# A macaron block on one core: value products of two pairs in one group, one scaled distance table, a new order of the side work, and head and tail by halves

## The chip, the cores and the metric

The kernel runs on one core of a Trainium2 chip. Its engines work at the same time and wait for each other by semaphores: PE (TensorE, matrix products and transposes into PSUM), ACT (ScalarE), DVE (VectorE), POOL (GpSimd), and SP (SyncE), which here only issues DMAs. The metric is the device time of one execution in microseconds (us), less is better.

## The reference

The input x has 16 batches of 512 rows of 128 numbers (float32). A feed-forward part with spikes, an attention part and the feed-forward part again are added to it in turn, each on the layer-normalised rows:

```
x = x + 0.5 * ffn(layernorm(x))
x = x + attention(layernorm(x))
x = x + 0.5 * ffn(layernorm(x))

ffn(u):  h = relu(u W_fc^T)^2            # 128 -> 512
         y = h W_proj^T                  # 512 -> 128
         five steps: mem = 0.9 mem + y - [mem > 1];  count += [mem > 1]
         result: count / 5
attention(u):  16 heads of 64 numbers, q scaled by 1/8
         sim = q k^T - slope[h] * |i - j|,  future positions masked
         out = softmax(sim) v;  result: out w_out + b_out
```

The slopes are 2^(-0.5 (h+1)) for head h.

## The kernel before, in words

**Tiling.** All products that must be exact are made of a high and a low half (`product3`: three matmuls on operands of type fp32r, high by high, low by high, high by low). The high half is ACT's copy out of PSUM, the low half DVE's subtraction of it from the same PSUM. The sixteen heads are worked on as eight pairs. A batch is eight slots, one for each pair `s`, and a slot is six beats `k`. In beat k the pair's scores of one entry of TILES are made (query tile i of head h against all keys up to it; for the narrow ones both heads in one bank). There are three score banks, so PE can be three tiles ahead of DVE.

**One tile's way.** PE makes the scores (`scores`, L431 and L432); DVE adds the distance bias and takes the row's minimum of the negated scores in one custom instruction (`bias_max`, L654), from a table `alibi` of 16 heads; ACT takes the exponential and the row sum (`exps`, L936); two beats later DVE takes the reciprocal of the sum (`recip`, L663) and POOL multiplies by it (`norm`, L1089). In the slot after, PE turns the pair's probabilities (`turn`, L445, five groups of four 128x128 transposes, at beats TBEAT) into two alternating banks, and ACT copies each to a ring `probT` of ten (L947). In the slot after that, PE makes the value products of the pair (`pv`, L459): for four key tiles and two heads, matmuls that write 64 output partitions each. The result's halves (ACT L954, DVE L770) enter the accumulation with w_out (`accumulate`, L514 to L517, at ACCBEAT).

**Side work.** SIDE lists what PE does besides, as (slot, beat, kind, number, batch offset): q, k and v of the next pairs, the first feed-forward part of the next batch (t1, fc1, y1), its attention input (t2), and the turned output and last part of the batch before (ot, t3, fc3, y3), and the value products ("pv", here of pair s-2, one pair in each slot). The entries use two side banks in turn, so each waits until the entry two before it has been read. In each beat PEORDER says in which order PE does side work (D), turned tiles (T) and accumulations (A), after the scores; ACTORDER does the same on ACT. The lists SPIKE1, SPIKE3, LN1, LN2 and LN3 place the steps of spikes (`spike_step`, L709 to L717) and layer norms on DVE and POOL: the stats and their aggregate on DVE (L667, L672), rstd on POOL (L1100, L1102), the normalise on DVE (L687).

**Queries and keys by DMA.** A pair's halves are copied between partitions by SP (`place`), for each pair after its q_lo and k_lo: first those for head 1, whose scores come first, then, when these have landed, those for head 0. The order of q and k in SIDE sets the order of the DMAs.

**Head.** Weights are loaded and turned, and batch 0 goes through t1, fc1, y1, the spikes and t2 with nothing beside it (`chain`, `block_by_halves` on DVE: only the spike steps are by halves of the 512 columns, the second half five steps behind the first). ACT makes the high halves of the weights and the 16 tables of `alibi` (L1050). `keep_warm` are products that nobody reads.

**Tail.** After the last slot PE makes the value products of pair 6, turns pair 7 through the two turn banks, makes its value products, accumulates, turns the output, and the last feed-forward part runs with nothing beside it.

## Time and profile before

| | us |
|---|---|
| median of 3 runs | 1609.67 (1609.4 to 1611.03) |
| the profiled execution | 1611.76 |
| its span, first to last instruction | 1610.0 |

In the profile's lists a line such as "L459" is one of the kernel's source, "x16" how often the instruction ran in a row, PEld PE's loading of weights, and what stands behind "<-" in brackets is what ended the engine's idle time before the row. Matmuls overlap: what one costs is read from the distance of two starts, not from its duration. Times of rows are from the span's start.

### The profile page before, as it was taken

To read this page: it belongs to the slowest core of one execution; us is meant where nothing else is said; L and a number is where in the kernel's file an instruction comes from. 1 tells how busy PE (TensorE), PEld (TensorE's weight loads), DVE (VectorE), ACT (ScalarE), POOL (GpSimd) and SP (SyncE) were. 2 spreads that over 40 slices of the span, in tenths; PEclk is the share of its full clock that TensorE was granted. 3 is DMA by queue.
4 is the path that set the end of the run, shared out by engine and by line. 5 is a ranking of instruction groups with operands and counts; after the bars stand their busy time and mean duration, and the time that the engine had idled before them with its cause. 6 is when DMAs were issued, how large, how long until landed. Compare 5 with 4: busy or idle time off the path is not lost.

```text
span 1610.0 us, 33997 instructions
## 1 busy us (share of the span) xinstructions
PE 1558.1 (97%) x10376; PEld 1253.8 (78%) x10376; DVE 1288.1 (80%) x4344; ACT 1312.4 (82%) x3485; POOL 954.2 (59%) x1253
## 2 busy tenths in 40 slices
PE   6899999999999999999999999999999999999996
PEld 5778778788787878778788787878778788787775
DVE  6586797878879788797878879788797878878765
ACT  6788888888888888888888888888888888888882
POOL 2555656666566666656666566666656666665551
PEclk8999999999999999999999999999999999999998
DMA  2454544444545444544444545444545444545440
GB/s 87 99 109 102 112 96 105 106 100 101 119 96 112 104 94 102 119 96 105 106 100 103 116 96 115 104 92 102 119 96 107 104 104 101 109 96 109 106 89 14
DMA packets 80052, 163.12 MB, mean 101 GB/s; under 512 B 12800, under 2 KB 30848, under 8 KB 79744
## 3 DMA queue, kind: packets, MB, share of 16 engines
q1 hardware_dynamic: 79872, 160.94, 46.4%
q8 instruction: 86, 1.41, 0.4%
q14 instruction: 94, 0.77, 0.1%
HBM read 6.88 MB, written 4.19 MB: 7 GB/s over the span
## 4 chain that ended last, share of the span: by engine, by line
PE 86%; DVE 9%; issue 2%; POOL 1%; ACT 1%; DMA 0%; POOLq 0%; DVEq 0%; SPq 0%; ACTq 0%
PE bank L445 16%; PE bank L459 14%; PE bank L431 11%; PE bank L432 10%; PE bank L411 7%; PE bank L415 7%; PE bank L412 7%; PE bank L504 7%; DVE xn L687 3%; PE bank L487 2%; PE bank L517 2%; PE bank L515 2%; PE bank L514 2%; DVE negsc L654 2%; POOL rstd L1102 1%
## 5 line engine op out<-in xcount | busy, mean ns | idle before, releaser
L1089 POOL TENSOR_TENSOR prob<-prob,rsum 128x512 f32<-128x512 f32 (+3 forms) x1024 | 769.9, 767 | 489.5 <-DVE rsum L663 486.9
L936 ACT ACTIVATE prob<-negsc,negmax 128x512 f32<-128x512 f32 (+3 forms) x1024 | 574.4, 563 | 165.7 <-DVE negmax L654 163.3
L654 DVE CUSTOM_DVE_ANT_0 negsc<-bank,alibi 128x512 f32<-128x512 f32 (+3 forms) x1024 | 466.9, 475 | 0.3 <-PE bank L432 0.3
L947 ACT COPY probT<-bank 128x512 f32<-128x512 f32 x640 | 352.0, 584 | 27.5 <-PE bank L445 21.4
L445 PE MATMUL bank<-ident,prob 128*128 128x128 f32 x2560 | 350.9, 273 | 0.8 <-POOL prob L1089 0.5
L431 PE MATMUL bank<-keys,queries 128*128 128x256 f32 (+2 forms) x1024 | 348.6, 351 | 0.3
L663 DVE RECIPROCAL rsum<-sums 128x1 f32<-128x1 f32 (+1 forms) x768 | 122.3, 159 | 260.1 <-PE bank L432 248.0
L432 PE MATMUL bank<-keys,queries 128*128 128x256 f32 (+2 forms) x1024 | 320.0, 324 | 0.0
L445 PEld LDWEIGHTS bank<-ident,prob 128*128 128x128 f32 x2560 | 299.4, 140 | 24.0 <-POOL prob L1089 0.7
L459 PE MATMUL bank<-probT,vals 128*64 128x512 f32 (+3 forms) x2048 | 303.9, 439 | 3.3 <-DVE queries L778 2.5
L459 PEld LDWEIGHTS bank<-probT,vals 128*64 128x64 f32 x2048 | 135.6, 136 | 163.6 <-issue 125.2
L431 PEld LDWEIGHTS bank<-keys,queries 128*128 128x128 f32 x1024 | 193.5, 189 | 33.1 <-issue 18.2
L432 PEld LDWEIGHTS bank<-keys,queries 128*128 128x128 f32 x1024 | 194.2, 190 | 15.1
L936 ACT ACTIVATION_READ_ACCUMULATOR prob<-negsc,negmax 128x1 f32 x1024 | 196.1, 191 | 0.0
L1095 POOL TENSOR_TENSOR hid<-hid 128x512 f32<-128x512 f32 x120 | 124.9, 1041 | 23.6 <-ACT hid L994 23.5
L504 PE MATMUL bank<-wproj,hid 128*128 128x128 f32 x1024 | 125.1, 275 | 0.3 <-DVE k_lo L785 0.3
L504 PEld LDWEIGHTS bank<-wproj,hid 128*128 128x128 f32 x1024 | 121.4, 192 | 2.7 <-DVE k_lo L785 0.7
L954 ACT CAST att_hi<-bank 128x512 fp32r<-128x512 f32 x128 | 74.8, 585 | 38.3 <-PE bank L459 37.5
L785 DVE TENSOR_TENSOR k_lo<-bank,keys 128x512 fp32r<-128x512 f32 x127 | 87.5, 689 | 8.5 <-ACT keys L969 7.9
L770 DVE TENSOR_TENSOR att_lo<-bank,att_hi 128x512 fp32r<-128x512 f32 x128 | 87.7, 685 | 5.2 <-ACT att_hi L954 5.2
L711 DVE SCALAR_TENSOR_TENSOR spikes<-negmem,spikes 128x512 f32<-128x512 f32 (+1 forms) x136 | 91.2, 673 | 0.8
L778 DVE TENSOR_TENSOR queries<-bank,queries 128x512 fp32r<-128x512 f32 x127 | 86.3, 680 | 4.6 <-ACT queries L969 4.0
(108 smaller groups left out, 2421.0 us busy)
## 6 DMA issues: line engine op xcount, KB each, us to landing
queries<-queries SPq DMA_DIRECT2D x381, 256.0 KB, 3.0
keys<-k_lo SPq DMA_DIRECT2D x254, 128.0 KB, 2.7
keys<-keys SPq DMA_DIRECT2D x127, 128.0 KB, 3.1
x_in<-in_L_attn_x_dram SPq DMA_DIRECT2D x16, 256.0 KB, 3.1
out_dram<-x SPq DMA_DIRECT2D x15, 256.0 KB, 3.6
prob<-in_L_attn_w_qkv_dram SPq DMA_DIRECT2D x1, 1536.0 KB, 9.4
prob<-in_L_attn_w_out_dram SPq DMA_DIRECT2D x1, 512.0 KB, 10.2
probT<-in_L_ffn_W_fc_dram SPq DMA_DIRECT2D x1, 256.0 KB, 3.3
```

The costliest lines, as they stand in the source:

```text
L411: pe.matmul(dst, w_hi, m_hi, start=True, stop=False)
L431: pe.matmul(dst, q_hi[:, p % 2, h, rows], keys[:, p % 2, h, 0:width], start=True, stop=False)
L432: mm = pe.matmul(dst, q_lo[:, p % 2, h, rows], keys[:, p % 2, h, 0:width], start=False, stop=True)
L445: mm = pe.transpose(turn_bank[n % 2][:, col:col + P], prob[:, p % 2, h, PCOL[i] + j * P:PCOL[i] + (j + 1) * P], ident[:, :])
L459: mm = pe.matmul(bank[h * DH:(h + 1) * DH, j * P:N], vals[:, (p // 2) % 2, j, (p % 2) * P + h * DH:(p % 2) * P + (h + 1) * DH], probT[:, t ...
L504: mm = pe.matmul(dst[:, t * C:(t + 1) * C], hid[:, i, rows], wproj[:, i, :], start=(i == 0 and t == 0), stop=(i == FC - 1), skip_group_che ...
L654: ins = dve.tensor_tensor_reduce(negsc[:, k % 3, col:col + WIDTH[i]], src, alibi[:, 2 * p + h, N - WIDTH[i]:N], 1.0, MASKED, ALU.add, ALU.min,
L663: dve.reciprocal(rsum[:, p % 2, cols], sums[:, p % 2, cols]).then_inc(s_rsum, 1)
L936: ins = act.activation(prob[:, p % 2, h, PCOL[i]:PCOL[i] + WIDTH[i]], negsc[:, k % 3, col:col + WIDTH[i]], ACT.Exp, bias=negmax[:, p % 2, ...
L947: act.copy(probT[:, turn_slot(p, t), :], turn_bank[(len(TRUNS) * p + t) % 2][:, :]).then_inc(s_turned_out, 1)
L1089: ins = pool.tensor_tensor(pr, pr, rsum[:, p % 2, seg:seg + 1].to_broadcast([P, WIDTH[i]]), ALU.mult)
L1095: pool.tensor_tensor(hid[:, i, :], hid[:, i, :], hid[:, i, :], ALU.mult).then_inc(s_hid[w], 1)
```

## The change

Value products: `pv` stands twice at one beat of the odd slots, for pairs s-3 and s-2, in place of once in every slot, and the ring `probT` has 20 places in place of ten. The distance table: one table `dist`, to which the scores are added; q's weights are divided by the head's slope beforehand and DVE's instruction multiplies by the slope. The order of side work, turned tiles, accumulations, spikes and layer norms is new. In head and tail the feed-forward part runs by halves of 256 columns on all engines, the squares of the second half on POOL; the second half of the spikes is seven steps behind. In the tail the last five turned tiles go to five banks, two of them are copied by DVE, and the last pair's value products, accumulation and output turn are by halves. The core of the diff:

```diff
-TRING = 10
+TRING = 20
 TBEAT = [
-    [1, 2, 2, 5, 5],
-    [1, 1, 3, 3, 5],
-    [1, 1, 4, 5, 5],
-    [1, 2, 4, 5, 5],
-    [1, 2, 2, 5, 5],
-    [0, 2, 3, 4, 5],
-    [1, 1, 4, 5, 5],
-    [1, 1, 3, 3, 5],
+    [1, 2, 3, 4, 4],
+    [1, 4, 4, 5, 5],
+    [1, 4, 4, 5, 5],
+    [1, 1, 4, 4, 5],
+    [3, 3, 4, 5, 5],
+    [0, 2, 2, 5, 5],
+    [1, 1, 4, 4, 5],
+    [0, 2, 2, 5, 5],
 ]
-ACCBEAT = [7, 6, 6, 6, 6, 6, 11, 11]
-OUTEV = (2, 1)
+ACCBEAT = [11, 15, 6, 17, 8, 11, 6, 8]
+OUTEV = (2, 3)
...
 SIDE = [
-    (0, 0, "q", 0, 0), (0, 1, "k", 0, 0), (0, 2, "v", 0, 0), (0, 4, "pv", 0, 0), (0, 4, "v", 1, 0),
-    (0, 5, "t1", 0, 1),
-    (1, 0, "q", 0, 0), (1, 1, "k", 0, 0), (1, 2, "fc1", 0, 1), (1, 4, "fc1", 1, 1), (1, 4, "pv", 0, 0),
-    (1, 5, "fc1", 2, 1),
-    (2, 0, "fc1", 3, 1), (2, 0, "k", 0, 0), (2, 1, "ot", 0, -1), (2, 2, "y1", 0, 1), (2, 3, "q", 0, 0),
-    (2, 4, "y1", 1, 1), (2, 4, "pv", 0, 0), (2, 5, "v", 0, 0), (2, 5, "t3", 0, -1),
-    (3, 0, "q", 0, 0), (3, 1, "k", 0, 0), (3, 3, "v", 1, 0), (3, 4, "pv", 0, 0), (3, 5, "fc3", 0, -1),
-    (4, 0, "k", 0, 0), (4, 1, "q", 0, 0), (4, 3, "v", 0, 0), (4, 4, "pv", 0, 0), (4, 5, "v", 1, 0),
-    (4, 5, "fc3", 1, -1),
-    (5, 0, "q", 0, 0), (5, 1, "k", 0, 0), (5, 3, "fc3", 2, -1), (5, 4, "pv", 0, 0), (5, 5, "fc3", 3, -1),
-    (6, 0, "k", 0, 0), (6, 1, "y3", 0, -1), (6, 1, "q", 0, 0), (6, 3, "y3", 1, -1), (6, 4, "pv", 0, 0),
-    (6, 4, "t2", 0, 1),
-    (7, 0, "q", 0, 1), (7, 1, "v", 0, 0), (7, 2, "k", 0, 1), (7, 3, "pv", 0, 0), (7, 4, "v", 1, 0),
+    (0, 0, "q", 0, 0), (0, 1, "v", 0, 0), (0, 2, "v", 1, 0), (0, 2, "k", 0, 0), (0, 3, "t1", 0, 1),
+    (0, 5, "fc1", 0, 1), (0, 5, "fc1", 1, 1),
+    (1, 1, "q", 0, 0), (1, 2, "k", 0, 0), (1, 4, "pv", 0, 0), (1, 4, "pv", 1, 0),
+    (2, 0, "q", 0, 0), (2, 1, "fc1", 2, 1), (2, 2, "k", 0, 0), (2, 3, "fc1", 3, 1), (2, 4, "v", 2, 0),
+    (2, 4, "ot", 0, -1),
+    (3, 0, "v", 3, 0), (3, 0, "k", 0, 0), (3, 1, "q", 0, 0), (3, 3, "pv", 0, 0), (3, 3, "pv", 1, 0),
+    (3, 5, "v", 4, 0),
+    (4, 0, "y1", 0, 1), (4, 0, "k", 0, 0), (4, 1, "y1", 1, 1), (4, 1, "t3", 0, -1), (4, 2, "q", 0, 0),
+    (4, 3, "fc3", 0, -1), (4, 4, "fc3", 1, -1), (4, 5, "fc3", 2, -1), (4, 5, "v", 5, 0),
+    (5, 1, "k", 0, 0), (5, 1, "q", 0, 0), (5, 3, "fc3", 3, -1), (5, 4, "pv", 0, 0), (5, 4, "pv", 1, 0),
+    (6, 0, "q", 0, 0), (6, 0, "k", 0, 0), (6, 3, "y3", 0, -1), (6, 3, "v", 6, 0), (6, 4, "y3", 1, -1),
+    (6, 4, "t2", 0, 1), (6, 5, "v", 7, 0),
+    (7, 1, "q", 0, 1), (7, 2, "k", 0, 1), (7, 4, "pv", 0, 0), (7, 4, "pv", 1, 0),
 ]
-SPIKE1 = [(2, 4), (3, 2), (3, 4), (3, 4), (4, 0), (4, 1), (4, 2), (4, 4), (4, 5), (5, 0), (5, 4), (5, 4), (6, 0), (6, 1)]
-SPIKE3 = [(6, 4), (6, 4), (7, 0), (7, 1), (7, 1), (7, 2), (7, 3), (7, 3), (7, 5), (8, 4), (9, 0), (9, 1), (9, 2), (9, 4)]
-LN1 = dict(stats=(0, 0), aggregate=(0, 3), rstd=(0, 3), normalise=(0, 4))
-LN2 = dict(stats=(6, 1), aggregate=(6, 2), rstd=(6, 2), normalise=(6, 4))
-LN3 = dict(stats=(2, 2), aggregate=(2, 4), rstd=(2, 4), normalise=(2, 4))
+SPIKE1 = [(4, 2), (4, 3), (4, 3), (4, 4), (4, 5), (4, 5), (4, 5), (4, 5), (5, 1), (5, 2), (5, 2), (5, 3), (5, 3), (5, 4)]
+SPIKE3 = [(7, 1), (7, 1), (7, 4), (7, 4), (7, 4), (8, 2), (8, 3), (8, 5), (9, 1), (9, 2), (9, 3), (9, 4), (9, 4), (9, 4)]
+LN1 = dict(stats=(0, 0), aggregate=(0, 1), rstd=(0, 2), normalise=(0, 2))
+LN2 = dict(stats=(5, 4), aggregate=(6, 2), rstd=(6, 3), normalise=(6, 4))
+LN3 = dict(stats=(3, 0), aggregate=(3, 1), rstd=(3, 1), normalise=(3, 2))
 FIRST = [(1, "q"), (1, "k"), (0, "q"), (0, "k")]
...
+        def pv_pair(b, s, i):
+            return before(b, s, 3 - i)
...
+        def last_turn_bank(t):
+            return turn_bank[(len(TRUNS) * (PAIRS - 1) + t) % 2] if t < 2 else score_bank[t - 2]
+        LAST_BY_VECTOR = (2, 4)
+        def acc_at(p):
+            return divmod((p - p % 2 + 3) * BEATS + ACCBEAT[p], BEATS)
         def score_col(k, n):
...
+            def block_by_halves(w, b, made):
+                e = 0 if w == 1 else 1
+                first = s_first_half
+                def turn_half(half):
+                    pe.wait_ge(*((first["xn"], e + 1) if half == 0 else (s_xn[w], b + 1)))
+                    for t in range(half * NT // 2, (half + 1) * NT // 2):
+                        mm = pe.transpose(end_turn_bank[half][:, t * P:(t + 1) * P], xn[:, t, :], ident[:, :])
+                    mm.then_inc(first["xT"] if half == 0 else s_xT[w], 1)
+                def fc_half(i, half):
+                    cols, rows = HALVES[half], slice(i * P, (i + 1) * P)
+                    low_made = None
+                    if i == 0:
+                        pe.wait_ge(*((first["xhi"], e + 1) if half == 0 else (s_xhi[w], b + 1)))
+                        low_made = (first["xlo"], e + 1) if half == 0 else (s_xlo[w], b + 1)
+                    if half == 1:
+                        pe.wait_ge(first["relu"], e * FC + i + 1)
+                    product3(end_fc_bank[i][:, cols], wfc_hi[:, rows], wfc_lo[:, rows], xf_hi[:, cols], xf_lo[:, cols],
+                             low_made).then_inc(first["fc"] if half == 0 else s_fc[w], 1)
+                def y_half(half):
+                    for i in range(FC):
+                        pe.wait_ge(*((first["hid"], e * FC + i + 1) if half == 0 else (s_hid[w], b * FC + i + 1)))
+                        for t in range(2):
+                            rows = slice((2 * half + t) * P, (2 * half + t + 1) * P)
+                            mm = pe.matmul(end_y_bank[half][:, t * C:(t + 1) * C], hid[:, i, rows], wproj[:, i, :],
+                                           start=(i == 0 and t == 0), stop=(i == FC - 1), skip_group_check=True)
+                    mm.then_inc(s_y[w], 1)
+                turn_half(0)
+                turn_half(1)
+                if made:
+                    pe.wait_ge(*made[0])
+                for i in range(FC):
+                    fc_half(i, 0)
+                if made:
+                    pe.wait_ge(*made[1])
+                y_half(0)
+                for i in range(FC):
+                    fc_half(i, 1)
+                y_half(1)
             def head():
...
                         keep_warm(6)
-                chain(0, ("t1",))
-                keep_warm(5)
-                pe.wait_ge(s_wfc_lo, 1)
-                chain(0, ("fc1",))
-                pe.wait_ge(s_wproj_out, 1)
-                chain(0, ("y1",))
-                pe.wait_ge(s_x1, 1)
-                keep_warm(9)
-                chain(0, ("t2",))
-                keep_warm(5)
+                block_by_halves(1, 0, ((s_wfc_lo, 1), (s_wproj_out, 1)))
+                pe.wait_ge(s_block_half, 1)
+                keep_warm(9, score_bank[1])
+                for half in range(2):
+                    pe.wait_ge(*((s_first_half["xn2"], 1) if half == 0 else (s_xn[2], 1)))
+                    for t in range(2 * half, 2 * half + 2):
+                        mm = pe.transpose(end_turn_bank[half][:, t * P:(t + 1) * P], xn[:, t, :], ident[:, :])
+                    mm.then_inc(s_first_half["xT2"] if half == 0 else s_xT[2], 1)
+                    keep_warm(3, score_bank[1])
...
+            def last_turn(t):
+                b, p = B - 1, PAIRS - 1
+                pe.wait_ge(s_norm, tile_no(b, p, TNEEDS[t]))
+                if t < 2:
+                    pe.wait_ge(s_turned_out, turn_no(b, p, t - 2))
+                elif t == 2:
+                    pe.wait_ge(s_biased, tile_no(b, p, BEATS - 1))
+                col = 0
+                for h, j in TRUNS[t]:
+                    for i in range(j, NT):
+                        mm = pe.transpose(last_turn_bank(t)[:, col:col + P],
+                                          prob[:, p % 2, h, PCOL[i] + j * P:PCOL[i] + (j + 1) * P], ident[:, :])
+                        col += P
+                mm.then_inc(s_turned, 1)
+            def last_pv(half):
+                b, p, end = B - 1, PAIRS - 1, HALVES[half].stop
+                pe.wait_ge(s_turned_out, turn_no(b, p, len(TRUNS) - 1))
+                pe.wait_ge(s_vals, v_no(b, p // 2, 1))
+                for j in range(2 * half + 2):
+                    start = max(j * P, HALVES[half].start)
+                    for h in range(2):
+                        t, col = place_of(h, j)
+                        mm = pe.matmul(last_pair_bank[half][h * DH:(h + 1) * DH, start:end],
+                                       vals[:, (p // 2) % 2, j, (p % 2) * P + h * DH:(p % 2) * P + (h + 1) * DH],
+                                       probT[:, turn_slot(p, t), col + start - j * P:col + end - j * P], start=(j == 0),
+                                       stop=(j == 2 * half + 1), skip_group_check=True)
+                mm.then_inc(s_pv, 1)
+            def last_accumulate(half):
+                b, p, cols = B - 1, PAIRS - 1, HALVES[half]
+                pe.wait_ge(s_att, pair_no(b, p) + half)
+                if half == 1:
+                    pe.wait_ge(s_outT, B)
+                pe.matmul(out_bank[:, cols], wo_hi[:, p, :], att_hi[:, p % 2, cols], start=False, stop=False, skip_group_check=True)
+                pe.matmul(out_bank[:, cols], wo_lo[:, p, :], att_hi[:, p % 2, cols], start=False, stop=False, skip_group_check=True)
+                pe.wait_ge(s_attlo, pair_no(b, p) + half)
+                pe.matmul(out_bank[:, cols], wo_hi[:, p, :], att_lo[:, p % 2, cols], start=False, stop=True,
+                          skip_group_check=True).then_inc(s_acc, 1)
+            def last_out_turn(half):
+                pe.wait_ge(s_outT, B + half)
+                for t in range(half * NT // 2, (half + 1) * NT // 2):
+                    mm = pe.transpose(turn_bank[half][:, t * P:(t + 1) * P], outT[:, t * P:(t + 1) * P], ident[:, :])
+                mm.then_inc(s_out, 1)
...
                     wait(pe, *last_user(len(SIDE) - (len(SIDE) - n) % 2, b, (-1, 0)))
-                for back in (3,):
-                    if ACCBEAT[PAIRS - 1] >= BEATS:
-                        accumulate(b, PAIRS - 3)
+                for p in range(PAIRS - 2):
+                    if acc_at(p) >= (PAIRS, 0):
+                        accumulate(b, p)
                 for j in PVORDER:
                     pv(side_bank[0], *six, j)
-                for t in range(3):
-                    turn(*seven, t)
+                for t in range(len(TRUNS)):
+                    last_turn(t)
+                for half in range(2):
+                    last_pv(half)
                 accumulate(*six)
-                for t in range(3, len(TRUNS)):
-                    turn(*seven, t)
-                for j in PVORDER:
-                    pv(side_bank[1], *seven, j)
-                keep_warm(6, score_bank[0])
-                accumulate(*seven)
-                keep_warm(4, score_bank[0])
-                out_turn(turn_bank[0], b)
-                keep_warm(16)
-                chain(b, ("t3",))
-                keep_warm(5)
-                chain(b, ("fc3", "y3"))
+                for half in range(2):
+                    last_accumulate(half)
+                    last_out_turn(half)
+                keep_warm(14, score_bank[1])
+                block_by_halves(3, b, None)
...
-                                                   alibi[:, 2 * p + h, N - WIDTH[i]:N], 1.0, MASKED, ALU.add, ALU.min,
+                                                   dist[:, N - WIDTH[i]:N], SLOPES[2 * p + h], MASKED, ALU.add, ALU.min,
...
+            def normalise_by_halves(w, src, b):
+                e = 0 if w == 1 else 1
+                dve.wait_ge(s_rstd[w], b + 1)
+                if w == 3:
+                    dve.wait_ge(s_xT[1], B)
+                    dve.wait_ge(s_xT[2], B)
+                for t in range(NT):
+                    ins = dve.tensor_scalar(xn[:, t, :], src[:, t, :], meanvar[:, w - 1, t, 0:1],
+                                            rstd[:, w - 1, t:t + 1], ALU.subtract, ALU.mult)
+                    if t == 1:
+                        ins.then_inc(s_first_half["xn"], 1)
+                ins.then_inc(s_xn[w], 1)
+                for half, cols in enumerate(HALVES):
+                    dve.wait_ge(*((s_first_half["xhi"], e + 1) if half == 0 else (s_xhi[w], b + 1)))
+                    dve.tensor_tensor(xf_lo[:, cols], end_turn_bank[half][:, cols], xf_hi[:, cols].bitcast(F32),
+                                      ALU.subtract).then_inc(s_first_half["xlo"] if half == 0 else s_xlo[w], 1)
+                for i in range(FC):
+                    dve.wait_ge(s_first_half["relu"], e * FC + i + 1)
+                    part = hid[:, i, HALVES[0]]
+                    dve.tensor_tensor(part, part, part, ALU.mult).then_inc(s_first_half["hid"], 1)
             def head():
...
+                for t in LAST_BY_VECTOR:
+                    dve.wait_ge(s_turned, turn_no(b, PAIRS - 1, t))
+                    dve.wait_ge(s_pv, pv_no(b, PAIRS - 5, NT - 1))
+                    dve.tensor_copy(probT[:, turn_slot(PAIRS - 1, t), :], last_turn_bank(t)[:, :]).then_inc(s_turned_out, 1)
...
-                chain(0, ("t1", "fc1", "y1"))
+                ends_by_halves(1, 0)
                 act.wait_ge(s_wqkv, 16)
-                act.mul(wq_hi[:, :], w_raw[:, 0:INNER], -SCALE).then_inc(s_whi, 1)
+                for h in range(HEADS):
+                    cols = slice(h * DH, (h + 1) * DH)
+                    ins = act.mul(w_raw[:, cols], w_raw[:, cols], -SCALE / SLOPES[h])
+                ins.then_inc(s_scaled, 1)
+                act.wait_ge(s_scaled, 1)
+                act.copy(wq_hi[:, :], w_raw[:, 0:INNER]).then_inc(s_whi, 1)
...
                 act.wait_ge(s_wlo, 1)
                 copy_twice("q", 1, wq_lo)
-                chain(0, ("t2",))
...
+            def square_second(w, b):
+                for i in range(FC):
+                    pool.wait_ge(s_relu[w], b * FC + (i + 1))
+                    half = hid[:, i, HALVES[1]]
+                    pool.tensor_tensor(half, half, half, ALU.mult).then_inc(s_hid[w], 1)
...
```

## Rows read from the trace of the kernel before

**Rows 1.** page, part 1: busy us, share of the span and instructions of each engine

```profile
PE 1558.1 (97%) x10376; PEld 1253.8 (78%) x10376; DVE 1288.1 (80%) x4344; ACT 1312.4 (82%) x3485; POOL 954.2 (59%) x1253
```

**Rows 2.** windows: stage, its us, busy us of each engine, granted clock, DMA share, GB/s

```profile
36.52:73.62 37.10, 31.94 (x191) 26.70 (x190) 21.30 (x86) 25.89 (x70) 21.02 (x27) 0.91 0.42 89
...
225.35:321.86 96.51, 95.63 (x644) 76.96 (x642) 79.93 (x270) 80.88 (x217) 59.72 (x79) 1.00 0.49 105
248.49:263.61 15.12, 15.12 (x112) 13.00 (x110) 10.22 (x40) 11.40 (x32) 9.96 (x14) 1.00 0.32 70
...
1570.10:1610.00 39.90, 26.03 (x183) 20.32 (x181) 23.70 (x62) 10.59 (x25) 4.99 (x8) 0.90 0.05 14
```

**Rows 3.** timeline of PE around one value group: start us, us, instruction

```profile
485.54 0.60 PE L445 MATMUL bank<-ident,prob 128*128 128x128 f32 x4
486.07 2.37 PE L459 MATMUL bank<-probT,vals 128*64 128x512 f32 x16
488.37 0.39 PE L431 MATMUL bank<-keys,queries 128*128 128x256 f32 x1
488.60 0.28 PE L432 MATMUL bank<-keys,queries 128*128 128x256 f32 x1
488.71 0.28 PE L431 MATMUL bank<-keys,queries 128*128 128x256 f32 x1
...
492.29 1.05 PE L445 MATMUL bank<-ident,prob 128*128 128x128 f32 x8
493.17 1.95 PE L504 MATMUL bank<-wproj,hid 128*128 128x128 f32 x16
```

**Rows 4.** waits, 200 to 1400 us: us in total, times, longest

```profile
PE bank L487 <- DVE xn L687: 9.2, 13, 0.7
...
PE bank L487 <- DVE att_lo L770: 2.2, 13, 0.2
```

**Rows 5.** timelines of PE, DVE and POOL around t2, 398 to 407 us

```profile
405.81 0.63 PE L487 MATMUL bank<-ident,xn 128*128 128x128 f32 x4 [0.71 <-DVE xn L687]
403.16 2.51 DVE L687 TENSOR_SCALAR xn<-x,meanvar,rstd 128x128 f32<-128x128 f32 x4
400.99 0.20 POOL L1100 TENSOR_TENSOR vareps<-meanvar,eps 128x4 f32<-128x4 f32 x1 [2.39 <-DVE meanvar L672]
...
402.25 2.82 POOL L1089 TENSOR_TENSOR prob<-prob,rsum 128x512 f32<-128x512 f32 x3
```

**Rows 6.** timeline of the head: the normalise of t2

```profile
29.34 1.11 DVE L687 TENSOR_SCALAR xn<-x,meanvar,rstd 128x128 f32<-128x128 f32 x4 [1.19 <-POOL rstd L1102]
```

**Rows 7.** DMA issues with KB and us to landing; and part 5's group of k_lo

```profile
keys<-k_lo SPq DMA_DIRECT2D x198, 128.0 KB, 2.7
...
L785 DVE TENSOR_TENSOR k_lo<-bank,keys 128x512 fp32r<-128x512 f32 x127 | 87.5, 689 | 8.5 <-ACT keys L969 7.9
```

**Rows 8.** waits, 1500 to 1515 us, in the last batch

```profile
PE bank L459 <- DVE queries L778: 1.5, 1, 1.5
PE bank L411 <- DVE x L758: 1.1, 1, 1.1
```

**Rows 9.** head: one row of the timeline, then of the chain: start us, us

```profile
21.70 8.42 ACT L1050 ACTIVATE alibi<-probT 128x512 f32<-128x512 f32 x16
15.24 0.38 ACT ysb L1003
...
25.43 0.42 DVE x L731
```

**Rows 10.** chain of the tail

```profile
1585.21 0.46 PE bank L523 x4
...
1589.11 1.12 DVE xn L687 x4
...
1597.06 0.38 ACT ysb L1003
...
1599.87 0.20 DVE spikes L709
```

273 lines of the change are left out of this document (171 added, 102 removed).

## The prediction

> **What bounds the kernel now.** I read the page's busy shares first, then the windows by stage, then PE's timeline around one value group, then the waits, the chain of the first 37 us and of the last 40 us. PE is busy 97% of the span [rows 1]. A steady batch takes 96.5 us, of which PE is busy 95.6 at full granted clock, DVE 79.9, ACT 80.9, POOL 59.7 [rows 2]: PE bounds the loop, the others follow within a tile or so, and a change is worth what it takes from PE's own time or from its idle moments. Three stretches have other limits: the head (to 36.5 us, a chain through all engines), the first slots (36.5 to 73.6, PE busy 31.9 of 37.1 us at a granted clock of 0.91) and the last 39.9 us, where PE is busy 26.0 [rows 2].
>
> **Value products of two pairs in one group.** These matmuls write 64 output partitions each, all others 128. Their 16 matmuls have 2 x 2 x (512+384+256+128) = 5120 columns, 2.13 us at 2.4 GHz, the level of this stretch (granted clock 1.00). From [rows 3]: start to start the group takes 488.37 - 486.07 = 2.30, 0.17 too much. The four transposes before it take 486.07 - 485.54 = 0.53, while eight elsewhere take 493.17 - 492.29 = 0.88, so four should take 0.44: 0.09 too much. The first 256-wide score after it takes 0.23, the next ones 0.11: 0.12 too much. In all 0.38. Some of the 0.17 may belong to the matmuls and not to the change of shape, so the bounds are 0.21 (nothing inside the group) and 0.38; the sum over the two borders is what repeats in every group, so I take 0.35. Going in and out is paid once per group. There are 128 groups now (8 pairs x 16 batches). After, the pairs go two by two at beats (1,4), (3,3), (5,4), (7,4): 3 groups in the first batch, 4 in each of the other 15, and two in the tail, 65. 63 x 0.35 = 22.1 us less (13 to 24).
>
> The Trainium skill ("TensorEngine Tiling (Array Packing)", Key Properties) says that changing the tiling mode, not just the tile, drains the engine. By that rule the pair boundary inside a double group costs nothing, since both pairs use the same mode. No row of this trace shows two such groups back to back.
>
> **The moved side work.** Each kind of side unit has as many entries as before (8 q, 8 k, 8 v, 4 fc1, ...), so PE's work is the same but for the borders. What changes is who waits. (a) PE waits at t2 for the normalised rows: 9.2 us in 13 batches, and at t1 for att_lo: 2.2 us in 13 [rows 4], 0.88 us a batch. At t2 DVE's normalise took 2.51 us for four tiles [rows 5], while in the head, with POOL idle, four take 1.11 [rows 6]. In between POOL ran three softmax scalings back to back, 2.82 us, because it had waited 2.39 us for meanvar at the rstd step just before [rows 5]. The change puts the aggregate one beat before rstd, so that backlog goes: one scaling (2.82 / 3 = 0.94) is left beside the normalise. DVE starts at 403.16 as before; 402.25 + 0.2 + 0.94 = 403.4, + 1.11 = 404.5, + 0.14 (405.81 less the end of the normalise, 405.67) = 404.6. PE arrives at t2 after two turned tiles (0.88) and a y unit (1.7 to 1.8, in place of the group's 2.30 and one turned tile), from 402.2 at about 404.9. So the t2 wait goes; with the old contention it would be 0.9. I take 0.1. At t1 the normalise now stands at (0,2) and t1 at (0,3), with no value group between them. Counted from the end of the group at (7,4), PE issues five tiles of scores up to there, five turned tiles, two accumulations, q, k and two v: 8.6 us (0.11 for 128 columns, 0.12 for 256 [rows 3], twice that for 512). DVE gets its scores at 2.8 and has three biases, stats, aggregate, q's low half and a spike step before the normalise, four wide ones of about 0.65 (k_lo's took 0.69 with its start-up [rows 7]) and smaller ones: 4.3, so it starts at 7.1; with 0.35 for one scaling on POOL, 1.11 and 0.14 the rows are ready at 8.7, and at 9.7 with 2.51 in place of 1.11 and no 0.35: a wait of 0.1 to 1.1, and 0 to 1.3 with my error in 15 operations. I take 0.4, near the lower end, because POOL has then one scaling to do. Sum 0.5 a batch in place of 0.88: 15 x 0.4 = 6 us less (13 less to 20 more).
> (b) In even slots there is no group now, and slot 2 falls from 15.1 [rows 2] to about 10 us (a group and two y units, 6, leave it); odd slots keep PE 4.6 us from the scores. Three score banks lie between PE and DVE. Spike steps are heaped: four at (4,5), finish and LN2 stats at (5,4). Over those beats DVE has up to 3 us more work than PE; before it is about 1.6. A third bank allows about two beats of 2 us, so I take no stall; up to 1 us a batch (15) is kept for the range.
> (c) k moves to beat 2 in slots 0, 1, 2 and 7, so its low half and the copy to the other partitions start later before the next pair's scores. A copy of k_lo takes 2.7 us to land, and DVE's subtraction 0.69 [rows 7]. In slot 2 PE does scores of three tiles, fc1, four turned tiles, v and ot after k: 4.9 us. The chain is a copy on ACT of about the same 0.7, DVE 0.9 with its bias ahead, DMA 2.7: 4.4 us with the semaphores. It just fits. It is SP's queue: the q copies stand ahead of k's where q comes first.
> (d) In the last batch PE waited 1.1 us for x2 and 1.5 for queries behind it [rows 8], since `ot` stood one beat after the accumulation of pair 7. Now ACT copies at (2,3) and `ot` stands at (2,4), behind a v: 2.6 less (0 to 3).
> (e) The first batch: slots 0 to 2 lose a group and two y units (2.3 + 3.6 us of PE work) to later slots, where PE is full, while PE idles here (5.2 of 37.1 us [rows 2]). Against that t1's wait is shorter by about 2 us and so is the slow clock behind it. I take 0 (3 less to 4 more).
>
> **DVE's bias operation** is the same instruction with a scale other than 1.0 and another second operand of the same size: 0 (nothing in it changes length). The 16 products that made the table took ACT 8.42 us of the head [rows 9]; in their place come 16 narrow ones on w_raw (estimate 4 us, half as long, each a fixed part and an eighth of the width) and one more 1024-wide copy (about 1 us). ACT's 3 us less matter only if ACT is last there.
>
> **Head.** Now: y's first half leaves ACT at 15.62, x1 is done at 25.85 [rows 9], scores start at 36.5 [rows 2]. By halves: fc on 256 columns halves the time to the first y: ready about 13.6, 2.0 earlier. But the second half's squares go to POOL, beside DVE's spike steps. Four squares of half width (0.6 each, estimated from 0.94 for a wide POOL operation [rows 5]) alternating with DVE's steps of 0.42 [rows 9]: second half ready at 17 to 18.5, and 13 steps and two sums later, of which six pairs interleave at 0.67 and seven stand alone, x1 is done at 24.4 to 26.1. LN2 by halves saves 0.5, the low-half subtraction of q and k for one pair only instead of two of 1.2 us saves about 1. I take 3.5 less (1 to 5).
>
> **Tail.** Five banks let the five last turned tiles follow without waiting for copies, two of the copies go to DVE: now the out turn is at 1585.21, rows normalised by 1590.23, y's first half at 1597.44, second spike half at 1599.87 [rows 10]. From the last score: the out turn about 1.5 to 2 earlier; fc and y by halves 3 earlier for the first half, but the store waits for the second, which has POOL's squares in it. From its start to the end stays 10 us. One accumulation (0.7) moves into the tail. 3.8 less (1 to 6).
>
> On POOL beside DVE: normalise took 2.51 against 1.11 [rows 5, 6]. The Trainium skill ("SBUF — State Buffer", SBUF: two separate sides) says the port pair that both share is an exclusive lock, held for a whole instruction. The trace agrees. By it the squares and spike steps in head and tail alternate and the second halves gain almost nothing: then head and tail give 2 us together, not 7.3.
>
> **Sum**, against the profiled execution's own 1611.8 us (span 1610.0): 22.1 + 6 + 2.6 + 0 + 3.5 + 3.8 = 38.0 less, 1573.8. The median of the runs shown is 2.1 below the profiled one: 1571.7, say 1572.
>
> **Rivals.**
> A, the new order adds waits: t1 at its upper bound (1.3 + 0.9 at t2, 1.3 more than now) or the DVE heap of (4,5): for it, DVE's excess nearly doubles; against it, DVE waits for PE now in most beats. +1 us a batch instead of -0.4: 21 more than forecast, 1593. Chance 0.17.
> B, the group's borders are cheaper to PE than counted or also paid between pairs (the change doesn't do what it says): 22 less gain, 1594. Against it: one row has both borders outside the group. 0.05.
> C, slower than before: the copy chain of (c) becomes the bound. If k_lo lands 3.7 instead of 2.7 us after issue and DVE is 1 us late, the next pair's scores wait 1.5 us in each of slots 0 and 2, from the point where the chain passes 4.9 us. To be slower it must cost over 38 / 15 = 2.5 us a batch; 3 gives 1572 + 45 = 1617. For it: the slack is 0.5 us. Against: a late PE also gives DVE time. 0.05.
> D, PE waits nowhere in the loop and the halves bring all: 15 x 0.5 more and 4 in head and tail, 1560. 0.15.
> By the lock rule of the page alone: 5 us above the forecast, 1577, inside it.
>
> **Numbers.** The forecast (1565 to 1583) has 0.58. Range 1558 to 1595: it takes in A, B and D. This kernel's measurement tells 0.2%, about 3.2 us, from no change. Faster by more: 0.93; within: 0.02; slower: 0.05.
>
> **What would show it.** PE's value groups in x32 with 4.4 to 4.6 us each and one slow first score behind them; a steady batch of 94.4 to 95; PE's wait for normalised rows under 0.3 us at t2; the first score at about 33; the last 40 us at 36 to 37. Wrong if PE's waits for DVE or for the copies grow past 1 us a batch, or the borders don't shrink in number.

## The result, and the profile after

The changed kernel takes 1626.13 us (median of 4, 1625.4 to 1627.7), the kernel before in the same session 1609.86: a ratio of 1.0100 (95% interval 1.0087 to 1.0114), 1.0% slower. The forecast was 1572, so 54 us are missing. The forecast's own signs of being wrong came true: PE's waits grew by 1.74 us a batch, where 1 was the sign, and a steady batch is 97.4 us long instead of 94.4 to 95. The profiled execution has a span of 1625.9 us against 1610.0, and 15.9 is what has to be explained.

By the first scores of each batch the span divides into (before, after): up to the first scores 36.52, 35.26; the first batch 92.3, 97.3; batches 2 to 15 1351.6, 1363.6 (96.54 and 97.40 each); the last batch to its slot 7 80.3, 80.3; the rest 49.2, 49.4. The head gained 1.3 and the tail lost 0.2; what was lost, was lost in the loop, 5.0 in the first batch and 12.0 in the next 14, where about 28 were forecast to be gained.

First the page's busy times (compare [rows 1]), then the windows by stage ([rows 2]): its us, then busy us of PE, PEld, DVE, ACT and POOL, granted clock, DMA share, GB/s. The third window is no stage of the forecast: it is beats (4,3) to (5,4) of batch 6.

```profile
PE 1554.5 (96%) x10365; PEld 1255.0 (77%) x10365; DVE 1281.2 (79%) x4353; ACT 1292.1 (79%) x3496; POOL 976.7 (60%) x1263
```

```profile
35.26:72.36 37.10, 29.90 (x162) 24.58 (x163) 21.78 (x91) 27.27 (x76) 23.95 (x32) 0.91 0.46 96
228.80:326.01 97.21, 95.31 (x644) 77.15 (x641) 79.51 (x269) 79.87 (x218) 61.07 (x78) 1.00 0.48 103
573.00:590.00 17.00, 16.24 (x98) 12.60 (x98) 16.83 (x43) 13.05 (x34) 12.18 (x13) 1.00 0.42 91
...
1586.00:1625.90 39.90, 25.53 (x177) 20.44 (x175) 27.88 (x70) 10.32 (x27) 7.91 (x11) 0.88 0.05 14
```

DVE has no more to do in a batch than before, 79.5 us of 97.2; of the other engines only POOL is clearly busy longer (61.1 us, before 59.7), because some of its operations now take longer. But in the 17 us from (4,3) to (5,4) DVE is busy 16.83; before it was busy 12.25 in the 15.0 us from 569.0, the same beats. Over a batch it has 18 us to spare, here none. That is the place, and the waits of PE from 200 to 1400 us say the same (in total, times, longest; before, two groups of them, 9.2 and 2.2 us [rows 4]):

```profile
PE bank L465 <- POOL prob L1287: 10.0, 12, 1.1
PE bank L479 <- ACT hid L1161: 4.6, 13, 0.4
PE bank L507 <- DVE xn L793: 3.7, 12, 0.3
PE bank L451 <- issue: 3.1, 5, 1.0
PE bank L537 <- DVE att_lo L878: 2.8, 9, 0.3
```

Slots and beats in brackets are those of PE's order. For a finer ledger I took, for batches 2 to 15, each distance between two starts on PE less the distance usual for that form, where it exceeds 0.15 us, by slot and beat. Before: 0.77 us a batch at t2 (6,4), 0.34 at t1 (0,5), 1.13 in all. After: **1.02 at (5,2)**, where a turned tile (L465) waits for POOL's scaled probabilities; **0.52 at (5,4)**, where the second pair's products (L479) wait for ACT's `hid` to free their bank; 0.44 at t1 (0,3); 0.30 at (2,0), accumulate on att_lo; 0.57 for landings of copied queries and keys ahead of scores (the profile calls most of them "issue"); 2.87 in all. So 1.74 more in waits and 1.4 less in borders; the batch is 0.86 longer, and the 0.5 between is what follows a wait (a remainder, not measured).

How the wait at (5,2) comes about, in one batch: DVE, then POOL, then PE (start, us, instruction, idle before).

```profile
577.59 1.07 DVE L817 SCALAR_TENSOR_TENSOR spikes<-negmem,spikes 128x512 f32<-128x512 f32 x1
...
579.07 1.04 DVE L820 SCALAR_TENSOR_TENSOR drive<-negmem,ysb 128x512 f32<-128x512 f32 x1
580.15 1.20 DVE L823 SCALAR_TENSOR_TENSOR negmem<-negmem,drive 128x512 f32<-128x512 f32 x1
581.38 1.41 DVE L817 SCALAR_TENSOR_TENSOR spikes<-negmem,spikes 128x512 f32<-128x512 f32 x1
582.72 0.68 DVE L820 SCALAR_TENSOR_TENSOR drive<-negmem,ysb 128x512 f32<-128x512 f32 x1
583.32 0.15 DVE L769 RECIPROCAL rsum<-sums 128x2 f32<-128x2 f32 x1
```

```profile
578.08 1.49 POOL L1293 TENSOR_TENSOR hid<-hid 128x512 f32<-128x512 f32 x1
579.53 1.27 POOL L1287 TENSOR_TENSOR prob<-prob,rsum 128x384 f32<-128x384 f32 x1
580.76 1.48 POOL L1293 TENSOR_TENSOR hid<-hid 128x512 f32<-128x512 f32 x1
583.55 1.18 POOL L1287 TENSOR_TENSOR prob<-prob,rsum 128x256 f32<-128x256 f32 x2 [1.31 <-DVE rsum L769]
```

```profile
584.79 1.09 PE L465 MATMUL bank<-ident,prob 128*128 128x128 f32 x8 [0.65 <-POOL prob L1287]
```

The four spike steps of beat (4,5) (579.07 to 582.72) stand ahead of the reciprocal at 583.32. One takes 0.68 us where POOL idles (582.72) and 1.04 to 1.41 beside POOL's operations, which are stretched too: the squares (L1293) have a mean of 1.30 us against 1.04 before. POOL then waits 1.31 us for the reciprocal, and PE for POOL. The rows show the two taking turns: each of the three long steps ends 0.54 or 0.55 us after an operation of POOL ends (579.57, 580.80 and 582.24). Before, spike steps and squares seldom met: from 200 to 1400 us 12 of 300 steps overlapped a square, after 84 of 293. In these lists the shortest, median and longest duration in ns stand behind the count; before, then after:

```profile
L711 DVE SCALAR_TENSOR_TENSOR spikes<-negmem,spikes x100: 673/684/730, 201.5 to 1390.9; 128x512 f32<-128x512 f32 x100
L1095 POOL TENSOR_TENSOR hid<-hid x97: 1036/1041/1047, 203.0 to 1361.6; 128x512 f32<-128x512 f32 x97
```

```profile
L817 DVE SCALAR_TENSOR_TENSOR spikes<-negmem,spikes x98: 674/693/1417, 200.8 to 1394.6; 128x512 f32<-128x512 f32 x98
L1293 POOL TENSOR_TENSOR hid<-hid x97: 1034/1487/1492, 202.7 to 1371.4; 128x512 f32<-128x512 f32 x97
```

The border, the one large gain, came as forecast: two pairs in 270.90 - 266.45 = 4.45 us, less than twice the 2.30 that one group took before [rows 3]: the change from one pair to the next costs nothing.

```profile
266.45 4.53 PE L479 MATMUL bank<-probT,vals 128*64 128x512 f32 x32
270.90 0.39 PE L451 MATMUL bank<-keys,queries 128*128 128x256 f32 x1
271.13 0.28 PE L452 MATMUL bank<-keys,queries 128*128 128x256 f32 x1
```

In the first batch PE waits longest at the end of slot 1, first SP's issue, then PE. The copy of k_lo (subtracted at 51.16) is issued at 52.50 behind the queries' and the high half's, and the scores start at 57.51; after that idle time the granted clock is 0.50 (1.2 GHz) for the 5.5 us to 63.0. The low clock is not new: over the first slots the mean is 0.91 before and after.

```profile
52.50 1.23 SPq L373 DMA_DIRECT2D keys<-k_lo  x1
```

```profile
52.56 1.12 PE L465 MATMUL bank<-ident,prob 128*128 128x128 f32 x8 [1.03 <-ACT probT L1114]
57.51 0.77 PE L451 MATMUL bank<-keys,queries 128*128 128x512 f32 x1 [3.84 <-issue]
```

The chain of the tail ([rows 10]): the output is turned at 1598.42, yet x2 comes at 1601.07, behind five steps left over of batch 15's third block. DVE had idled 3.08 us up to 1592.71, waiting for turned tiles of PE; experiment 4 takes them there.

```profile
1597.59 0.59 DVE spikes L817
...
1600.35 0.70 DVE x L829
1601.07 0.43 DVE x L1074
...
1611.34 0.37 ACT ysb L1203
...
1616.38 0.29 DVE spikes L815
```

### The profile page after: what moved, and what is told of

It reads as the page before. It is cut to its first block, busy times and chain, and to the rows that moved or that the text cites. A ratio compares the mean times of both kernels' runs of the same rounds, so it can differ in the third digit from the quotient of the medians.

```text
span 1625.9 us, 33995 instructions
## 1 busy us (share of the span) xinstructions
PE 1554.5 (96%) x10365; PEld 1255.0 (77%) x10365; DVE 1281.2 (79%) x4353; ACT 1292.1 (79%) x3496; POOL 976.7 (60%) x1263
## 3 DMA queue, kind: packets, MB, share of 16 engines
q8 instruction: 86, 1.41, 0.4%
## 4 chain that ended last, share of the span: by engine, by line
PE 67%; DVE 21%; issue 5%; ACT 4%; DMA 1%; POOL 0%; SPq 0%; DVEq 0%; ACTq 0%; POOLq 0%
PE bank L479 13%; PE bank L465 11%; PE bank L451 8%; PE bank L452 7%; PE bank L524 7%; PE bank L431 5%; PE bank L435 5%; PE bank L432 5%; DVE negsc L760 4%; DVE drive L820 3%; DVE spikes L817 3%; ACT prob L1103 3%; DVE negmem L823 2%; DVE xn L793 2%; PE bank L537 2%
## 5 line engine op out<-in xcount | busy, mean ns | idle before, releaser
L1287 POOL TENSOR_TENSOR prob<-prob,rsum 128x512 f32<-128x512 f32 (+3 forms) x1024 | 756.0, 754 | 570.4 <-DVE rsum L769 570.0
L760 DVE CUSTOM_DVE_ANT_0 negsc<-bank,dist 128x512 f32<-128x512 f32 (+3 forms) x1024 | 466.6, 474 | 0.1
L465 PE MATMUL bank<-ident,prob 128*128 128x128 f32 x2540 | 344.4, 274 | 13.1 <-POOL prob L1287 11.9
L465 PEld LDWEIGHTS bank<-ident,prob 128*128 128x128 f32 x2540 | 293.0, 140 | 41.0 <-POOL prob L1287 23.3
L479 PE MATMUL bank<-probT,vals 128*64 128x512 f32 x2032 | 290.7, 436 | 5.2 <-ACT hid L1161 5.0
L479 PEld LDWEIGHTS bank<-probT,vals 128*64 128x64 f32 x2032 | 135.6, 137 | 156.2 <-issue 117.0
L1103 ACT ACTIVATION_READ_ACCUMULATOR prob<-negsc,negmax 128x1 f32 x1024 | 202.7, 198 | 0.0
L1293 POOL TENSOR_TENSOR hid<-hid 128x512 f32<-128x512 f32 x120 | 155.1, 1297 | 0.3 <-ACT hid L1161 0.3
L524 PE MATMUL bank<-wproj,hid 128*128 128x128 f32 x960 | 116.9, 275 | 0.0
L524 PEld LDWEIGHTS bank<-wproj,hid 128*128 128x128 f32 x960 | 114.9, 192 | 1.3
L817 DVE SCALAR_TENSOR_TENSOR spikes<-negmem,spikes 128x512 f32<-128x512 f32 (+1 forms) x136 | 113.8, 837 | 2.4
L886 DVE TENSOR_TENSOR queries<-bank,queries 128x512 fp32r<-128x512 f32 x127 | 86.9, 684 | 15.9 <-ACT queries L1136 15.0
L823 DVE SCALAR_TENSOR_TENSOR negmem<-negmem,drive 128x512 f32<-128x512 f32 (+1 forms) x102 | 94.1, 922 | 0.7
```

What stands on the lines that cost most here:

```text
L465: mm = pe.transpose(turn_bank[n % 2][:, col:col + P], prob[:, p % 2, h, PCOL[i] + j * P:PCOL[i] + (j + 1) * P], ident[:, :])
L479: mm = pe.matmul(bank[h * DH:(h + 1) * DH, j * P:N], vals[:, (p // 2) % 2, j, (p % 2) * P + h * DH:(p % 2) * P + (h + 1) * DH], probT[:, t ...
L524: mm = pe.matmul(dst[:, t * C:(t + 1) * C], hid[:, i, rows], wproj[:, i, :], start=(i == 0 and t == 0), stop=(i == FC - 1), skip_group_che ...
L760: ins = dve.tensor_tensor_reduce(negsc[:, k % 3, col:col + WIDTH[i]], src, dist[:, N - WIDTH[i]:N], SLOPES[2 * p + h], MASKED, ALU.add, AL ...
L817: ins = dve.scalar_tensor_tensor(out=spikes[:, cols], in0=mem[:, cols], scalar=sign * THRESHOLD, in1=spikes[:, cols], op0=fires, op1=ALU.add)
L823: ins = dve.scalar_tensor_tensor(out=negmem[:, cols], in0=mem[:, cols], scalar=sign * THRESHOLD, in1=drive[:, cols], op0=fires, op1=ALU.su ...
```

## The experiments

Ratios are to the kernel before. "Heap" is the pile of spike steps at (4,5), "mended ends" the fourth run's edit. Lines start with the kernel's own names, edits are to the changed kernel.

**1. The borders.** One product of 128 columns on the full array, between the two pairs.

```diff
                 elif kind == "pv":
+                    if i == 1:
+                        pe.matmul(side_bank[n % 2][:, 0:P], ident[:, :], ident[:, :], start=True, stop=True)
                     for j in PVORDER:
                         pv(bank or side_bank[n % 2], *pv_pair(b, s, i), j)
```

> Edit: the changed kernel with one full-array product of 128 columns put between the two pairs' value products of every double group, which gives back the border that the change removed; nothing else is changed (63 of them). Border theory: a border in and out costs 0.35 us beside the product's own 0.10: 63 x 0.45 = 28 us more than the changed kernel, less what falls into waits that stand right behind it: 1648 to 1656 us, ratio 1.024 to 1.029, and the second pair's first gap is again 0.42 us and more. Rival, borders overlap with other work or with the weight load: only the product's own time, 63 x 0.10 = 6 us, 1630 to 1634.

1646.81 us, 1.0226 (1.0211 to 1.0241), 20.7 more than the changed kernel. That is less than expected, since PE's waits fell from 2.87 to 2.25 a batch. The timeline shows the border itself. From 200 to 1400 us the stretch from the first value product to the next score grew from 4.46 to 5.03 us in the 37 of 49 double groups that hold no wait, by 0.57:

```profile
248.49 2.37 PE L479 MATMUL bank<-probT,vals 128*64 128x512 f32 x16
250.80 0.49 PE L565 MATMUL bank<-ident 128*128 128x128 f32 x2
251.22 2.38 PE L479 MATMUL bank<-probT,vals 128*64 128x512 f32 x16
253.52 0.38 PE L451 MATMUL bank<-keys,queries 128*128 128x256 f32 x1
```

The product is two records (x2). In the tail of the changed kernel 14 such products stand in a row, 28 records whose starts are 0.11 apart:

```profile
1599.96 3.29 PE L572 MATMUL bank<-ident 128*128 128x128 f32 x28
```

So the product itself is 0.22 (the expectation counted 0.10), and the border 0.57 - 0.22 = 0.35. The forecast's 0.35 stands, and the gain of about 22 us was there and was spent.

**2. Spreading the heap.**

```diff
-SPIKE1 = [..., (4, 4), (4, 5), (4, 5), (4, 5), (4, 5), (5, 1), (5, 2), (5, 2), (5, 3), (5, 3), (5, 4)]
+SPIKE1 = [..., (4, 4), (4, 5), (4, 5), (5, 1), (5, 2), (5, 3), (5, 4), (5, 4), (5, 4), (5, 5), (5, 5)]
-LN2 = dict(stats=(5, 4), ...
+LN2 = dict(stats=(6, 1), ...
```

> Edit: in the changed kernel the first block's spike steps are spread (two of the four at (4,5) move to (5,1), the rest follow down to (5,5)) and the second LayerNorm's statistics move from (5,4) to (6,1). Heap theory: the PE waits at (5,2) (turned tile on the normalised probabilities, 1.02 us a batch) and (5,4) (second value pair's group on the hidden half, 0.52) come from the pile of spike steps on VectorE between 4,5 and 5,2, each stretched by GpSimd's squares beside it (1.04 to 1.41 us where one takes 0.68 alone). Then both waits go, 1.5 us a batch, and with their followers up to 1.9: 15 batches give 20 to 28 us; some of it comes back as new waits further on. Expected 1600 to 1610 us, ratio to before 0.995 to 1.000. Rival, total load: VectorE and GpSimd have too much to do in the second half of the batch and the pile only moves: 1624 to 1630, waits of the same sum at (5,5) to (6,4).

1627.27 us, 1.0111 (1.0094 to 1.0128): nothing gained. (5,2) fell to 0.14 and (5,4) to nothing, but 0.56 came at (6,1), 0.56 at t2 and 0.49 at (6,4) for a bank; 2.82 in all. The rival was right on the total.

```profile
PE bank L507 <- DVE xn L793: 8.5, 24, 0.4
PE bank L465 <- POOL prob L1287: 5.6, 15, 0.4
PE bank L524 <- ACT ysb L1170: 4.2, 13, 0.3
```

**3. Earlier queries and keys.** Slot 1: q (1,0), k (1,1); slot 2: k (2,1), fc1 (2,2).

> Edit: in slots 1 and 2 of the changed kernel the query and key tiles are made one beat earlier (slot 1: q at beat 0, k at beat 1; slot 2: k at beat 1, the third fc tile at beat 2). Copy theory: the key copies made by DMA from GpSimd's k_lo land 3.8 to 5 us after their issue, so with k at beat 2 the next slot's first scores wait for them: 0.44 us a batch at the ends of slots 1 and 2, and 4.0 us in the first batch at the end of slot 1, after which TensorE runs at the lower clock for some 6 us. Then 0.4 x 15 = 6 and in the first batch 4 to 6 more: 1614 to 1618 us, ratio 1.003 to 1.006. Rival, GpSimd: k_lo is late because GpSimd is still at the squares and attention remainders, so an earlier tile on TensorE changes nothing there: 1624 to 1628, waits at the same places.

1634.46 us, 1.0147 (1.0131 to 1.0162), 8 slower. That is outside both theories. The first batch gained 3.5 us, as the copy theory had it, and has no stretch at half clock in its first slots. A steady batch lost 0.61: PE waits 0.80 instead of 0.30 at (2,0) for att_lo. The last batch lost 3.2, with 6.8 us at a granted clock of 0.50 from 1548.4. (k_lo is made by DVE, not by GpSimd as the expectation says.)

**4. The ends.**

```diff
-                for n in spilled[:2]:
+                for n in spilled[:6]:
...
+                weights_low(1, wk_hi, wk_lo, others, s_wrest)
                 norm2_normalise(1)
-                weights_low(1, wk_hi, wk_lo, others, s_wrest)
+                weights_low(0, wq_hi, wq_lo, others, s_wrest)
```

> Edit: the ends of the changed kernel alone. In the head the rest of the key weights' remainders is subtracted ahead of the second half's normalise and the query weights' right behind it (they stood behind the second half's remainders of x, beside GpSimd's 3.3 us on the value weights, and one of them took 2.54 us). In the tail the spike steps left over are taken while VectorE is idle (six instead of two ahead of the last pair, the last ones right behind). Theory: head 1.5 to 2.5 us earlier (first scores at 33 to 34 instead of 35.26), tail 1.5 to 3 (x2 no longer at 1601.07 behind five steps): 1620.5 to 1623, ratio 1.006 to 1.009. Rival: what ends last in the head is the value weights on GpSimd, and in the tail the last turned tiles: 1625 to 1627.

1619.42 us, 1.0061 (1.0046 to 1.0076). The tail is 3.0 us shorter, as expected. The head is not shorter (first scores 35.2): the subtraction moved beside POOL's rstd, which took 1.43 us instead of 0.69, and the normalise waited for it. The first batch is 2.0 shorter and the steady ones 0.3 each, where only landings of copies differ; this I can't ascribe to the edit.

**5. Is it DVE's load?** On the mended ends; nothing is moved. The rest of six spike steps' columns in each steady batch is left out of the computation.

```diff
+                elif w == 1 and n > 3 and n % 3 != 0:
+                    cols = slice(0, 2)
```

> Edit: the changed kernel with the mended ends (1619.4 us), where six of the first block's fourteen spike steps in each steady batch (drive and membrane of the last three times) work on 2 columns instead of 512; the place and the order of everything stay. The rest of their columns is left out of the computation. It tells whether VectorE's load in slots 4 and 5 is what TensorE waits for at (5,2) and (5,4). Load theory: about 6 x 0.8 us less on VectorE before (5,4), more where GpSimd's squares stretch them; the waits at (5,2) 1.03 and (5,4) 0.52 a batch go, with 0.3 of followers: 1.5 to 1.9 us a batch, 1592 to 1598. Rival, GpSimd itself (squares of the third block ahead of its normalising, 1.3 us each): (5,2) stays for the most part, 1608 to 1616.

1591.69 us, 0.9881 (0.9865 to 0.9898), 27.7 less. The waits at (5,2) and (5,4) are gone, a steady batch takes 95.3 us, and three kinds of wait are left:

```profile
PE bank L507 <- DVE xn L793: 4.1, 13, 0.3
PE bank L537 <- DVE att_lo L880: 3.1, 10, 0.3
PE bank L451 <- issue: 2.9, 6, 1.0
```

POOL's squares were all still there, so the rival falls: DVE's load between (4,2) and (5,4) costs 1.85 us a batch. (This is the price of the load of the six steps where they stand, their turns with POOL included; the run doesn't divide the two. The kernel before has the same fourteen steps and no such wait.)

**6. y of the first block earlier.** Two value tiles go to slot 4 for it; one spike step to a beat from (3,3).

```diff
-    (3, 0, "v", 3, 0), (3, 0, "k", 0, 0), (3, 1, "q", 0, 0), (3, 3, "pv", 0, 0), (3, 3, "pv", 1, 0),
-    (3, 5, "v", 4, 0),
-    (4, 0, "y1", 0, 1), (4, 0, "k", 0, 0), (4, 1, "y1", 1, 1), (4, 1, "t3", 0, -1), ...
+    (3, 0, "y1", 0, 1), (3, 0, "k", 0, 0), (3, 1, "q", 0, 0), (3, 2, "y1", 1, 1), (3, 3, "pv", 0, 0), ...
+    (4, 0, "v", 3, 0), (4, 0, "k", 0, 0), (4, 1, "v", 4, 0), (4, 1, "t3", 0, -1), ...
```

> Edit: the changed kernel with the mended ends, and in it the first block's two y tiles a slot earlier (slot 3, beats 0 and 2, in the place of two value tiles, which go to slot 4), so that its fourteen spike steps stand one to a beat from (3,3) to (5,4); before this edit they stood from (4,2) to (5,4), in the kernel before from (2,4) to (6,1). Window theory (what is left of the heap theory after spreading within slots 4 and 5 had only moved the waits): the new order has put y of the first block so late that VectorE has 14 spike steps and the rest of its work in the 12 beats before the turned tile of the second LayerNorm at (6,4), and is behind whatever their order. With 27 beats as before it is not: the waits at (5,2), (5,4) and those that the spread moved to (6,1) and (6,4) go, 1.5 to 1.8 us a batch, 15 batches: 22 to 28 us less than 1619.4, so 1591 to 1598, ratio 0.989 to 0.993. Rival, GpSimd: the wait at (5,2) comes from the squares of the third block standing ahead of the normalising, and stays (1.0 us a batch): 1606 to 1613.

1648.47 us, 1.0239 (1.0217 to 1.0261). The theory's gain came, and a larger loss with it. The waits at (5,2), (5,4) and (6,4) went, and slot 5 fell from 14.2 to 12.7 us. But 2.36 a batch came at (4,1): a value tile wants the bank of the one two entries before, ACT has still to copy it, and ACT stands behind an exponential that waits for DVE. PE, then ACT:

```profile
580.88 0.39 PE L430 MATMUL bank<-wv_hi,xa_hi 128*128 128x256 f32 x1 [2.19 <-ACT vals L1141]
```

```profile
579.54 0.72 ACT L1102 ACTIVATE prob<-negsc,negmax 128x512 f32<-128x512 f32 x1 [0.84 <-DVE negmax L759]
...
580.26 0.56 ACT L1141 COPY vals<-bank 128x512 f32<-128x512 f32 x1
```

**7. The same with the banks set apart** (y at (3,0) and (3,1), q (3,2); slot 4: k, t3 and v, q), later third spikes.

> Edit: the mended ends, the late spike steps of the third block as in the run before this one, and the first block's y tiles at (3,0) and (3,1), its spike steps one to a beat from (3,3) to (5,4). In the first try of early y tiles two value tiles one beat apart had the same bank, and the second stood 2.36 us a batch waiting for ScalarE's copy of the first; here no two tiles of one bank are closer than that order had them elsewhere. What the first try had shown else: slot 5 12.7 us instead of 14.2 and no waits at (5,2), (5,4) or (6,4). Window theory: left are 4.96 less 2.36, 0.32, 0.24 and 0.5 of their followers, less 0.7 for the later spike steps: 0.9 us a batch, so 95.3 us a batch, 1590 to 1597, ratio 0.987 to 0.992. Rival, banks: with both side banks taken by a double group and two tiles needed in each beat of slots 3 and 4, some pair of tiles always meets; the wait moves to another tile of slots 3 and 4 (1 to 2 us a batch): 1610 to 1630.

1718.14 us, 1.0673 (1.0654 to 1.0692): the rival, and several times dearer than it said. The ledger has 8.17 us a batch, most of it for banks held until DVE's subtraction: 1.88 and 1.72 at (4,1) and (4,2), 1.51 at (3,3) ahead of the double group. Not all of it is waiting. PE's idle time is 5.9 a batch; most of the rest is PE at half clock, for 3.4 to 10.2 us in every steady batch, which no steady batch of the mended ends has:

```profile
600.00:606.80 6.80, 5.34 (x17) 4.24 (x18) 3.04 (x10) 2.22 (x5) 1.40 (x2) 0.50 0.18 39
```

From 200 to 1400 us the mean granted clock is 0.97, against 1.00 with the mended ends: about 3 of the 6.7 us that a batch lost (an estimate, 0.03 of 103.8). In experiment 6 it is 0.99.

**8. The double groups in the old order.** On the mended ends, with TBEAT, PEORDER, ACTORDER, the spikes and the first and second layer norms at the beats of the kernel before; only both pairs' products in the odd slots, `ot` at (2,4), t3 at (3,5); the accumulations and the first fc3 tile, at (4,2), moved with them.

> Edit: the grouping without the new order. The changed kernel with the mended ends, but the side work, the turned tiles, the order on TensorE and ScalarE, the spike steps and the first and second LayerNorms stand in the beats of the kernel before; only what the grouping forces is moved (both pairs' value products in slots 1, 3, 5 and 7, the output tile at (2,4), the turned tile of the third LayerNorm at (3,5)). Theory: the grouping itself is worth its borders, 1.4 us a batch, and the new order is what loses: then 1609.7 less 21, less 2 to 6 at the ends, plus what the waits at the double groups bring: 1582 to 1592, ratio 0.983 to 0.989. Rival, grouping itself is at fault: products for two pairs in one beat leave the other engines 2.1 us more to make up at a time, and the waits appear in this order too: 1605 to 1625.

1823.62 us, 1.1322 (1.1305 to 1.1338). This is the largest miss of the experiments, on the far side of both theories: 15.3 us of waits a batch.

```profile
PE bank L505 <- DVE xn L791: 44.2, 22, 2.3
PE bank L429 <- DVE att_lo L876: 22.3, 33, 0.8
PE bank L449 <- DMA queries<-queries: 20.2, 22, 1.4
```

The second line is the grouping's own: a double group fills both side banks, so an fc tile one beat behind it, (1,5) or (5,5), stands until att_lo is subtracted, 0.99 us each. The old order had a tile there, with one bank free. So the grouping can't simply be put into the old order; how the rest divides (xn at 2.5 and 1.85 a batch) these runs don't tell.

**9. Small moves.** The third block's steps from the sixth on later ((8,3), ..., the last two (9,5)), and keys of slots 1 and 2 at beat 1; then, without the keys, those steps and the last fc3 tile at (5,2); then with the heap spread, LN2 at (6,0) to (6,3) and y3 at (6,2) as well.

> Edit: the changed kernel with the mended ends (1619.4 us), and the small waits alone: the third block's last eight spike steps later (its sixth at (8,3) instead of (8,2), so behind the first LayerNorm's normalise; the last two at (9,5) instead of (9,4), so behind the remainder of the attention's output), the keys of slot 1 at beat 1 behind the queries, those of slot 2 at beat 1 with the fc tile behind them. Theory: each of the waits at (0,3) (0.44 a batch), (2,0) (0.35), and the late key copies (0.1 a batch, 2.75 us in the first batch) goes by itself: 0.9 x 15 + 3 = 16, so 1601 to 1606, ratio 0.995 to 0.998. Rival, waits move on to the next wait of TensorE, which stays at (5,2): a batch keeps 97.1 us, 1615 to 1619.

> Edit: the mended ends; the third block's spike steps from the sixth on as in the run with the three small waits (the sixth at (8,3), the last two at (9,5)), keys left where the change has them; and the third block's last fc tile at (5,2) instead of (5,3). In the run with the three small waits the spike steps had taken the waits at (0,3) and (2,0) away, and the earlier keys had brought 1.02 us a batch back at (2,2) and (2,3), where an fc tile waits for the bank of the tile two before it. Theory: without those keys 0.44 + 0.35 a batch stay gone, and the wait at (5,4) for the fc tile's bank (0.52) shrinks: 0.8 to 1.3 x 15 = 12 to 20 us less than 1619.4: 1600 to 1607. Rival, banks: the fc tile at (5,2) waits for the bank of the key tile of (5,1), 0.5 to 1.0 a batch: 1607 to 1615.

> Edit: as the run before this one, and the first block's spike steps spread down to (5,5) with no more than three in a beat, the second LayerNorm's steps at (6,0), (6,1), (6,2) and (6,3), and the third block's first y tile at (6,2) instead of (6,3). Spreading alone had taken 0.9 off the wait at (5,2) and brought 0.56 at (6,1), 0.56 at (6,4) for the second LayerNorm's x and 0.49 at (6,4) for a bank. Theory: with the LayerNorm a beat earlier and the y tile's bank free sooner the last two do not come: 0.5 to 1.5 us a batch less than the run before: 1585 to 1600. Rival, VectorE is behind by a fixed amount until (6,4) because y of the first block stands late (27 beats for its spike steps in the kernel before, 13 here): the waits stay 1.5 us a batch in sum wherever they fall, 1600 to 1610.

1627.45 us, 1.0101 (1.0082 to 1.0120); 1639.37, 1.0176 (1.0161 to 1.0191); 1627.50, 1.0098 (1.0080 to 1.0116). In each the wait aimed at went (t1's 0.44 in all; t2's and (6,1)'s in the third) and others came for banks: 0.64 and 0.38 at (2,2) and (2,3) in the first; about 1 at (5,2) for the bank of the key tile one beat before in the second and third; 0.98 at (6,2) in the third. The 0.64 at (2,2) stands in all three, also where the keys were left in place, so it isn't the keys', as the second expectation has it. What the three share, and experiments 4 and 10 without this wait don't have, are the two spike steps at (9,5), just ahead of the query's subtraction. Of the second:

```profile
PE bank L431 <- DVE k_lo L893: 10.6, 12, 0.9
PE bank L465 <- POOL prob L1287: 10.2, 12, 1.1
PE bank L431 <- DVE queries L886: 6.4, 11, 0.6
```

Two runs more stacked such moves on early y tiles (fc3 at (5,0), accumulate at (2,1); then keys): 1670.87 and 1687.11 us; and the seventh with earlier keys, 1730.55.

**10. Only DVE's steps moved.**

```diff
-SPIKE1 = [..., (4, 5), (4, 5), (4, 5), (4, 5), (5, 1), (5, 2), (5, 2), (5, 3), (5, 3), (5, 4)]
+SPIKE1 = [..., (4, 5), (4, 5), (5, 0), (5, 1), (5, 2), (5, 3), (5, 4), (5, 4), (5, 4), (5, 5)]
-SPIKE3 = [..., (8, 2), (8, 3), (8, 5), (9, 1), (9, 2), (9, 3), (9, 4), (9, 4), (9, 4)]
+SPIKE3 = [..., (8, 3), (8, 4), (8, 5), (9, 0), (9, 1), (9, 2), (9, 3), (9, 4), (9, 4)]
-LN2 = dict(stats=(5, 4), aggregate=(6, 2), rstd=(6, 3), normalise=(6, 4))
+LN2 = dict(stats=(6, 0), aggregate=(6, 1), rstd=(6, 2), normalise=(6, 3))
```

> Edit: the changed kernel with the mended ends, no side tile on TensorE moved; on VectorE the first block's spike steps spread down to (5,5) with no more than three in a beat, the second LayerNorm at (6,0) to (6,3), and of the third block's steps the sixth at (8,3) (behind the first LayerNorm's normalise) and the ninth on one beat earlier, so that two and not three stand at (9,4) ahead of the attention's remainder. What the runs so far say together: moves of side tiles (bank B free two beats later) brought 0.6 to 2.4 us a batch each, moves on VectorE alone took waits away: (0,3) 0.44 gone, (5,2) 1.03 to 0.14, (6,1) and the second LayerNorm's wait at (6,4) gone once the LayerNorm stands earlier. Theory: left are 0.14 at (5,2), 0 to 0.5 at (6,4) for the y tile's bank, 0 to 0.3 at (2,0), 0.2 of DMA landings: 0.6 to 1.2 us a batch against 2.62, with followers 1.6 to 2.3 less a batch: 1585 to 1597, ratio 0.985 to 0.992. Rival, fixed debt: VectorE is behind until the second LayerNorm whatever its order, waits stay at 2 us a batch: 1608 to 1618.

1604.29 us, 0.9965 (0.9951 to 0.9978): 0.35% faster than the kernel before, the best of all but experiment 5, which leaves work out, and 7 us short of the expected range. Against the mended ends a steady batch is 0.90 shorter, the first 4.3, and the last 1.5 longer. 1.56 us of waits a batch are left, of which 0.80 at (6,3) and 0.41 at (1,4), for banks that the query tile's subtraction holds.

```profile
PE bank L524 <- DVE queries L886: 8.3, 13, 0.6
PE bank L479 <- DVE queries L886: 5.0, 11, 0.5
```

**11. Two steps further.** The key tile of slot 1 a beat earlier; and LN2 at (6,1), (6,2), (6,2), (6,3) with the third spikes at (9,1), (9,2), (9,3), (9,3), (9,4), (9,4).

> Edit: as the one before, and the key tile of slot 1 at beat 1 behind the query tile instead of beat 2. Theory: in the first batch the scores of slot 2 wait 2.75 us less for the key copies, in the others 0.1: 2 to 4 us less than the one before. Rival: the key tile waits for the bank of the fc tile two before it (0.3 a batch): 2 to 5 us more.

> Edit: as the best so far (1604.3 us; no tile on TensorE moved, spike steps spread), with the second LayerNorm's statistics at (6,1) and its aggregate at (6,2), so that the remainders of the query and key tiles of slot 6 stand ahead of them, and the third block's steps at (9,1), (9,2), (9,3) twice, (9,4) twice instead of one each from (9,0). In the best so far TensorE waits 0.80 us a batch at (6,3) for a bank that the query tile's remainder holds behind those statistics, and 0.41 at (1,4) for one held by the query tile's remainder behind the step at (9,1). Theory: both go, 1.2 us a batch, 12 to 18 us: 1586 to 1593, ratio 0.985 to 0.989. Rival, debt: the LayerNorm is now late and TensorE waits for it at (6,4) instead, 0.6 to 1.2 us a batch: 1598 to 1606.

1607.84 us, 0.9985 (0.9976 to 0.9994), and 1623.84, 1.0085 (1.0071 to 1.0099). The first is 3.6 more, in the rival's range, though PE shows no wait for the bank that it names. In the second both waits went as meant, and 0.45 at t2, 0.48 at (6,4), 0.66 at (6,5) and 0.34 at (2,0) came back: 2.59 a batch, and 19.6 us more than experiment 10 by DVE's steps alone.

## Why the prediction was wrong

**Value groups: right.** 65 groups, 4.46 us for two pairs where PE doesn't wait inside (5.04 at (5,4), where it does), 0.35 a border; 63 x 0.35 = 22 us were gained.

**t1 and t2: right.** 0.44 and nothing a steady batch, forecast 0.4 and 0.1; 0.67 less than before. (The first batch waits 2.6 us at t2, before 1.65.) That t2 has no wait may in part be luck, since PE came there late from its waits in slot 5; but experiment 5, without those and with less for DVE to do, has none either.

**(b), "I take no stall": the step that failed.** The working compared DVE's excess over PE with the depth of the score banks ("a third bank allows about two beats of 2 us"), and its 3 us of excess are about four steps at the 0.7 that one takes alone. Two things were missed. The fourteen steps stand in the beats of POOL's four squares of the third block, and each makes the other wait: 1.0 to 1.4 us, a heap of 4.3 in place of 2.7. The exclusive port pair that the Trainium skill ("SBUF — State Buffer", SBUF: two separate sides) describes was applied in the prediction to head and tail. The trace agrees with it here too: of the 121 spike steps from 200 to 1400 us that took over 0.95 us and saw an operation of POOL end, all end 0.55 or 0.56 us after that end (before, 62 steps took so long, with the same distance). It should have been applied to this heap. Long steps alone are not what loses, though: in experiment 10 148 steps take over 0.95 us, and it is 15 us faster than the mended ends. What counts is what stands behind them. And what was late was not the scores, which three banks cover, but the reciprocal, from which a turned tile hangs over POOL, and the bank of the fc tile. Experiment 5 prices it at 1.85 us a batch, 27.7 in all, half of the 54 missing. Rival A had the place (the DVE heap of (4,5), +1 us a batch, 1593, chance 0.17), but its price was too small.

**The deeper form of the same error.** The window of the work was not read. y of the first block moved from (2,2) and (2,4) to (4,0) and (4,1) with t2 left at (6,4): from y's second tile to t2 are 15 beats, before 24 (the counts in the expectations are a little different). Spreading inside it only moved the wait (experiment 2), which speaks for a debt; a better order of DVE's steps took 1.1 of the 2.6 us of waits a batch off all the same, and 0.9 off the batch (experiment 10), so part is order. That y stands late because double groups fill both side banks is what experiments 6 to 8 suggest: each try to put it back ran into a bank, and the low clock followed the long waits. It is not shown that no order could.

**(c) copies: too small.** "It just fits" did not hold: 0.57 us a batch before scores, and 0.3 at (2,0) for att_lo, which was not in the working at all. **(e), taken as 0 (3 less to 4 more):** the first batch is 5.0 longer, outside even these bounds. k at beat 2 cost 3.84 us of idle time there; experiment 3 gave 3.5 us back.

**(d) the last batch:** the wait for x2 went, 2.6 us, but 1.49 at t3 and 1.45 at a key tile came in slot 4, as 0.71 in slot 0: the batch is no shorter.

**Head: 1.3 instead of 3.5.** The first y was ready at 13.98, near the 13.6 forecast. But the second half's squares on POOL, 0.69 to 0.79 us each, paced its products of y, which came in four lots 0.75 us apart, and x1 was done at 26.6, forecast 24.4 to 26.1 and before 25.9. What was gained came behind it, although the subtraction of wq took 2.54 us beside POOL's wv_lo. **Tail: nothing instead of 3.8.** Five leftover steps ahead of x2 (3.0 us, experiment 4) and POOL's squares: the second half's spikes start 4.6 us after the first's. The 1577 that the lock rule of the Trainium skill ("SBUF — State Buffer", SBUF: two separate sides) alone gave had 2 for both terms, and 1.1 came; that is partly luck, since the leftover steps have nothing to do with the lock, and with them mended head and tail give 4.1.

**Added up,** roughly, with what is small left out: 27.7 for the load of DVE, 12 for the new waits of (c) in the steady batches, 5 in the first batch, 6 at head and tail and 2.6 for (d) make 53 of the 54 us.

## What to carry to other kernels

Where work is moved between beats, check for each engine the window from the operation that feeds it to the one that needs it, and cost its instructions at the duration they have beside what the neighbour does in the same beats; a busy share of 79% over the batch hid 17 us without a gap. A gain that fills two buffers at once takes the slack of everything that uses them: list which entries stand a beat behind. Moving DVE's steps alone gave the only gain (15 us against the mended ends), but not surely: other orders gave nothing (experiment 2) or lost 19.6 us again (the second of 11). No run in which tiles moved in the ring of two banks gained by it: against the mended ends (in experiment 3 the changed kernel, in the first of 11 experiment 10) a steady batch was 0.2 to 7 us longer, and 14 in the old order; most moved steps of DVE as well. And look at the granted clock of such a run: part of what looks like waiting is PE at the lower clock behind the waits.

## What the runs showed of the hardware

A GpSimd operation and a VectorE operation with two inputs in SBUF took turns, and the one that began first took its usual time. In the head of the changed kernel the subtraction of wq (128x896, begun at 31.25 on VectorE) took 2.63 us by its row and ended 0.95 after GpSimd's wv_lo (29.75 to 32.93); in experiment 4, begun at 30.38 just ahead of GpSimd's (30.55), it took 1.09. The 128x2 power of rstd took 0.69 us with VectorE idle, and 1.43 in experiment 4, where VectorE's subtraction ran until 29.28. A duration in the profile holds the time an operation is kept waiting in this way, so such an engine looks busy.

A copy of k_lo lands in 2.4 us in the median. In the first batch, with four other copies issued from 50.69 to 54.90, the one of 52.50 had landed when SP issued the next at 57.44, 4.9 us later.

A full-array product of 128 columns (two records) between two half-width groups costs 0.57 us, against 0.22 in a row of such products.
